# Routing table of a mixture of experts built on the chip, in place of a scatter to HBM

## The reference, cut to what matters

```python
x = x + scan_layer(layernorm(x))                      # 8 sequences of 1024 tokens
xt = layernorm(x).reshape(8192, 256)
scores = softmax(xt @ gate_w.T)                       # 15 experts
topk_w, topk_idx = top_k(scores, 3); topk_w /= topk_w.sum(-1)
comb = zeros(8192, 15); comb[t, topk_idx] += topk_w
h  = einsum('td,efd->etf', xt, fc1_w) + fc1_b         # 15 x 512
a  = gelu(h[..., 256:]) * h[..., :256] * geglu_mult
y  = einsum('etd,te->td', a @ fc2_w.T + fc2_b, comb)
ys = shared_expert(xt)                                # the same form, 512 wide
out = x + y + ys
```

## Time and profile before

| | us |
|---|---|
| median of 3 runs | 1831.01 (1828.75 to 1833.40) |
| the profiled execution | 1831.13 |
| its span | 1829.3 |
| busy in the span: PE, DVE, ACT, POOL | 1484.2, 1081.9, 873.3, 1123.2 |
| POOL's scatters into the table, 192 | 193.7 busy, 152.7 idle before them |
| mean granted clock of TensorE | 0.915 |

### The profile page before, as it was taken

One profiled execution on the slowest core, in us unless ns is written; L12 is line 12 of the kernel. 1 busy time (PEld: TensorE's weight loads), 2 busy tenths in 40 slices (PEclk: granted clock), 3 DMA queues, 4 the chain that ended last, 5 costly groups with the idle time before them and its releaser, 6 DMA issues. The chain is left out here.

```text
span 1829.3 us, 24446 instructions
## 1 busy us (share of the span) xinstructions
PE 1484.2 (81%) x5592; PEld 894.7 (49%) x5592; DVE 1081.9 (59%) x2159; ACT 873.3 (48%) x1490; POOL 1123.2 (61%) x1005
## 2 busy tenths in 40 slices
PE   6893667677677499666994399999999999996997
PEld 3432444445444244333453166666666666664565
DVE  5655999999999354133653144444444444442698
ACT  6887989988998232112220133333333333332110
POOL 6887888888886256456675366666666666662000
PEclk9996888888889699888997599999999999998999
DMA  4333233333231589999897022222222222224895
GB/s 146 132 110 137 71 127 115 127 115 110 99 126 59 189 116 130 103 98 138 99 95 96 29 89 88 87 87 89 87 87 88 89 84 90 89 87 155 313 347 210
DMA packets 75225, 216.47 MB, mean 118 GB/s; under 512 B 19926, under 2 KB 20950, under 8 KB 75120
## 3 DMA queue, kind: packets, MB, share of 16 engines
q1 hardware_dynamic: 41664, 133.23, 27.4%
q0 software_dynamic: 27904, 61.06, 10.6%
q10 hardware_dynamic: 5552, 20.86, 8.0%
HBM read 147.89 MB, written 67.21 MB: 118 GB/s over the span
## 5 line engine op out<-in xcount | busy, mean ns | idle before, releaser
L1766 PE MATMUL bank<-arena_dt,xgT 128*128 x832 | 393.8, 596 | 0.1
L738 POOL TENSOR_TENSOR state<-arena_x,b_all 128x1024 f32<-128x1024 f32 x128 | 301.8, 2370 | 67.0 <-issue 64.5
L762 PE MATMUL bank<-ident,state 128*128 128x128 f32 x1024 | 202.4, 332 | 147.4 <-ACT scaled L675 71.2
L1721 POOL DMA_INDIRECT choice_out<-ye,ids x208 | 205.2, 987 | 163.3 <-DVE ye L1874 159.9
L817 DVE TENSOR_TENSOR_SCAN state<-bank,state 128x1024 f32<-128x1024 f32 x128 | 291.5, 2278 | 5.0 <-POOL state L738 4.9
L1860 DVE TENSOR_TENSOR hid<-bank,arena_x 128x512 f32<-128x512 f32 x208 | 143.8, 692 | 251.0 <-PE bank L1766 251.0
L1316 POOL DMA_INDIRECT row_table<-choice_all,row_i x192 | 193.7, 1009 | 152.7 <-DMA row_table<-choice_all,row_i 85.2
L762 PEld LDWEIGHTS bank<-ident,state 128*128 128x128 f32 x1024 | 158.0, 211 | 197.6 <-DVE state L817 111.2
L1712 POOL DMA_INDIRECT xg<-x_norm,tokens x208 | 201.3, 968 | 72.9 <-issue 60.9
L1832 ACT ACTIVATE gluT<-bank 128x256 f32<-128x256 f32 x208 | 79.9, 384 | 321.8 <-PE bank L1775 321.8
L1783 PE MATMUL bank<-arena_x,gluT 128*128 x832 | 213.9, 380 | 0.0
(11 more groups left out here) (180 smaller groups left out, 2202.4 us busy)
## 6 DMA issues: line engine op xcount, KB each, us to landing
b_all<-bc_rows SPq DMA_DIRECT2D x64, 512.0 KB, 3.6
arena_x<-choice_out SPq DMA_DIRECT2D x16, 1536.0 KB, 10.2
xin<-in_x SPq DMA_DIRECT2D x16, 512.0 KB, 3.6
x_skip<-xin SPq DMA_DIRECT2D x16, 512.0 KB, 2.6
y_acc<-x_skip SPq DMA_DIRECT2D x8, 1024.0 KB, 6.7
x_mid<-y_acc SPq DMA_DIRECT2D x8, 1024.0 KB, 6.5
arena_x<-x_mid SPq DMA_DIRECT2D x16, 512.0 KB, 27.3
x_norm<-arena_x SPq DMA_DIRECT2D x16, 512.0 KB, 30.8
```

The lines of the kernel that those rows point to most:

```text
L738: pool.tensor_tensor(state[j % STATES][:, :, here], gT[:, :, b, here], b_all[j % BUFS][:, here].unsqueeze(1).to_broadcast([P, KD, TH]), AL ...
L762: last = pe.transpose(bank[:, TURN + (BY_PE * j + q) % 2, i * D + k * P:i * D + (k + 1) * P], state[j % STATES][:, k, t // GT * CH + t % G ...
L1721: pool.indirect_dma_start(out=choice_out, out_offset=bass.IndirectOffsetOnAxis(ap=ids[:, j % 2, j // 2:j // 2 + 1], axis=0), in_=ye[c][:], ...
L1766: last = pe.matmul(bank[:, 2 + s, :], xgT[s][:, k, :], w1[:, k, ds(e_no * (2 * F), 2 * F)], start=(k == 0), stop=(k == KD - 1))
```

## The change

A row of the table is now addressed by column (expert x 8 + block of 128 rows modulo 8, 120 in all) and slot (row modulo 128). For each group DVE makes, in two halves of six choices per partition, one-hots of the slot, multiplied by the choice number plus one (`slot_hot`), and one-hots of the column (`column_hot`); `rows` splits the rank into slot and column for that, with four small instructions more; PE multiplies them, 12 products summed into a 120x128 part of PSUM bank 7 (`place`), which DVE copies out (`keep_out`). At the end, from the counts per group, DVE finds to which tile each group's column belongs (`blocks`, `tiles_of_blocks`), makes one-hots of that, and PE sums 16 products into the ids of all 208 tiles, transposed already. `scatter`, the table in HBM and its clearing are gone, and so are the two gathers and the transposes ahead of the experts. The one-hots and constants lie in b2's place and the copies partly in that of the last eighth of w1; so these two are loaded last, on ACT's queue, and the first `fc1` of the experts on PE and the first bias on DVE wait for them.

```diff
-                    def scatter(g):
-                        pool.wait_ge(rows_made, g + 1)
-                        for t in range(g * GT, (g + 1) * GT):
-                            wait(pool, c_sent[t % 4], 48 * (t // 4))
-                            for k in range(TOPK):
-                                pool.indirect_dma_start(
-                                    out=row_table, out_offset=bass.IndirectOffsetOnAxis(ap=row_i[:, t, k:k + 1], axis=0),
-                                    in_=choice_all[:, t, k:k + 1], in_offset=None).then_inc(c_sent[t % 4], 16)
@@ tensor, routing stage
-                    def rank(g):
+                    def rank(g, n_placed):
                         pe.wait_ge(seen_made, GT * (g + 1))
                         wait(pe, rank_read, g)
+                        wait(pe, out_kept, n_placed)
+                        pe.matmul(bank[0:E, 7, 64 + g:65 + g], seen[g % 2][:, 0, :], ones[:, 0:1], start=True, stop=True)
...
+                    def place(g, n_ranked):
+                        wait(pe, rank_read, n_ranked)
+                        wait(pe, out_kept, g)
+                        for h in range(2):
+                            pe.wait_ge(hots_made, 2 * g + h + 1)
+                            for m in range(HK):
+                                last = pe.matmul(bank[0:COLS, 7, P:2 * P], column_hot[h][:, m, :], slot_hot[h][:, m, :],
+                                                 start=(h == 0 and m == 0), stop=(h == 1 and m == HK - 1))
+                            last.then_inc(hots_read, 1)
...
                         for g in routed_at(q - 4):
-                            rank(g)
+                            rank(g, n_placed)
+                            n_ranked += 1
+                        for g in routed_at(q - 8):
+                            place(g, n_ranked)
+                            n_placed += 1
...
+                    pe.wait_ge(blocks_made, 1)
+                    pe.matmul(bank[0:COLS, 3, 0:GROUPS], same_expert, blocks_at[:, 0:GROUPS], start=True, stop=True)
...
+                    for g in range(GROUPS):
+                        pe.wait_ge(tiles_hot, g + 1)
+                        pe.matmul(bank[:, 5, 0:XT], ids_placed[g], tile_hot[g], start=(g == 0), stop=(g == GROUPS - 1))\
+                          .then_inc(tile_hot_read, 1)
@@ scalar, routing stage
-                            act.dma_start(b2[:, at], b2_row[at].partition_broadcast(P)).then_inc(w_loaded, 16)
-                        if q % 2 == 1 and 2 * W2N < q < 2 * W2N + 2 * W1N:
+                        if q % 2 == 1 and 2 * W2N < q < 2 * W2N + 2 * (W1N - 1):
...
+                    act.wait_ge(tile_hot_read, GROUPS)
+                    at = ds(last_w1, W1P)
+                    act.dma_start(w1[:, :, at], w1_rows[:, :, at]).then_inc(late_loaded, 16)
+                    act.wait_ge(ids_kept, 1)
+                    act.dma_start(b2[:], b2_row.partition_broadcast(P)).then_inc(late_loaded, 16)
@@ vector, routing stage
+                    def hots(g, h):
+                        dve.wait_ge(rows_made, g + 1)
+                        wait(dve, hots_read, 2 * g + h - 1)
...
+                        for m in range(HK):
+                            at = h * HK + m
+                            dve.tensor_scalar(slot_hot[h][:, m, :], number[:, 0:P], slot_block[g % 2][:, 0, at:at + 1],
+                                              choice_all[:, g * GK + at:g * GK + at + 1], ALU.is_equal, ALU.mult)
+                        dve.tensor_tensor(
+                            column_hot[h], number[:, 0:COLS].unsqueeze(1).to_broadcast([P, HK, COLS]),
+                            column[g % 2][:, h * HK:(h + 1) * HK].unsqueeze(2).to_broadcast([P, HK, COLS]), ALU.is_equal)\
+                            .then_inc(hots_made, 1)
+
+                    def keep_out(g):
+                        dve.wait_ge(hots_read, 2 * g + 2)
+                        dve.tensor_copy(ids_placed[g], bank[0:COLS, 7, P:2 * P]).then_inc(out_kept, 1)
...
+                    def tiles_of_blocks():
+                        dve.wait_ge(blocks_spread, 1)
...
+                        for g in range(GROUPS):
+                            wait(dve, tile_hot_read, g - HOTS + 1)
+                            dve.tensor_scalar(tile_hot[g], number[0:COLS, :], tile_of[:, g:g + 1], None, ALU.is_equal)\
+                               .then_inc(tiles_hot, 1)
...
+                    def read_ids():
+                        dve.wait_ge(tile_hot_read, GROUPS)
+                        table(dve.tensor_scalar(empty, bank[:, 5, 0:XT], 0.0, float(1 << 20), ALU.is_equal, ALU.mult))
+                        table(dve.scalar_tensor_tensor(ids_f, bank[:, 5, 0:XT], -1.0, empty, ALU.add, ALU.add))
+                        dve.tensor_copy(ids[:], ids_f).then_inc(ids_kept, 1)
...
                         for g in routed_at(q - 4):
                             rows(g)
+                        for g in routed_at(q - 8):
+                            keep_out(g)
...
                         for g in routed_at(q - 2):
                             choose(g)
                             if g + 3 < GROUPS:
                                 measure(g + 3)
                         if i == 3 and 0 <= j < G1:
                             add_bias(j)
+                        for h in range(2):
+                            for g in routed_at(q - 6 - h):
+                                hots(g, h)
@@ expert stage
-                    for s in range(2):
-                        pool.indirect_dma_start(
-                            out=row_ids[:, s, :], out_offset=None, in_=row_table.rearrange("(r p) o -> r (p o)", p=P),
-                            in_offset=bass.IndirectOffsetOnAxis(ap=tile_row[0:XT // 2, s:s + 1], axis=0)).then_inc(ids_loaded, 16)
...
+                    pe.wait_ge(late_loaded, 32)
                     e_of = {0: expert_of(0)}
                     fc1(0, 0, e_of[0])
...
+                    dve.wait_ge(late_loaded, 32)
                     add_bias(0, 0)
```

More of the change, by code:

```diff
@@ L1211, in model_kernel, with in_b2 @@
             wmul = sb("wmul", [P, KD, E])
-            RPP = (E + 1) * TILES // P
-            junk = sglu[1][:].rearrange("p k t -> p (k t)")[:, 0:RPP * P]
+            GK, RING_COLS = GT * TOPK, 8
+            HK, COLS = GK // 2, E * RING_COLS
+            row_i = sb("row_i", [P, GK], I32)
+            slot_block_i = sb("slot_block_i", [P, 2, GK], I32)
+            slot_block = [sb(f"slot_block{c}", [P, 2, GK]) for c in range(2)]
+            column = [sb(f"column{c}", [P, GK]) for c in range(2)]
+            room = [0]
+            def in_b2(shape, parts=P, dt=F32):
+                at, words = room[0], 1
+                for size in shape:
+                    words *= size
+                room[0] += words
+                assert room[0] <= E * D
+                return b2[0:parts, at:at + words]
+            slot_hot = [in_b2([HK, P]).rearrange("p (m c) -> p m c", m=HK) for _ in range(2)]
+            column_hot = [in_b2([HK, COLS]).rearrange("p (m c) -> p m c", m=HK) for _ in range(2)]
+            HOTS = room[0] // XT
+            tile_hot = [b2[0:COLS, (g % HOTS) * XT:(g % HOTS + 1) * XT] for g in range(GROUPS)]
+            empty, ids_f = b2[:, 0:XT], b2[:, XT:2 * XT]
+            number = in_b2([XT])
+            late_out = [in_b2([P], COLS) for _ in range(2)]
+            same_expert, lower_expert = in_b2([COLS], E), in_b2([COLS], E)
+            counts_at = in_b2([GROUPS + 1], E)
+            blocks_at = in_b2([GROUPS + 1], E)
+            first_block = in_b2([GROUPS + 1], COLS)
+            ahead_f = in_b2([GROUPS], COLS)
+            tile_of = in_b2([GROUPS], COLS)
+            ring_no = in_b2([1], COLS)
+            last_w1 = (W1N - 1) * W1P
+            ids_placed = [arena_dt[0:COLS, last_w1 + g * P:last_w1 + (g + 1) * P] for g in range(7)]
+            ids_placed += [arena_dt[0:COLS, E * 2 * F + last_w1 + g * P:E * 2 * F + last_w1 + (g + 1) * P] for g in range(7)]
+            ids_placed += late_out
+            assert len(ids_placed) == GROUPS and 7 * P <= W1P
             x2_loaded, xn2_stored, xm_loaded, stored = sems("x2_loaded", 4), sems("xn2_stored"), sems("xm_loaded"), sems("sh_stored")
@@ L1540, in choose @@
                         dve.wait_ge(index_made, g + 1)
-                        wait(dve, row_step, 2 * (g - 1))
+                        wait(dve, row_step, 5 * (g - 1))
                         dve.tensor_tensor(
@@ L1555, in rows @@
                     def rows(g):
-                        s, here = g % 2, slice(g * GT, (g + 1) * GT)
+                        s = g % 2
                         dve.wait_ge(ranked, g + 1)
[L1558 to L1562, removed]
@@ new lines, in rows @@
+                        if g == GROUPS - 1:
+                            dve.tensor_copy(counted[:], bank[:, 7, 96:96 + E])
+                            dve.tensor_scalar(counts_at[:, GROUPS:GROUPS + 1], bank[0:E, 7, 65 + g:66 + g], float(P - 1), None,
```

(19 more changed lines are left out.)

147 lines of the change are left out of this document (81 added, 66 removed).

## The result

The changed kernel takes 1865.32 us (median of 4 runs, 1861.96 to 1865.65), the kernel before in the same comparison 1829.88 (4 runs, 1825.27 to 1833.40): a ratio of 1.0191, 95% interval 1.0165 to 1.0217. The forecast was 1856 us, the range 1826 to 1882. The profiled execution takes 1861.96 us, its span is 1860.1.

What follows compares the result with a forecast made beforehand. The prediction took the loop to be bound by transfers crowded by 192 single-word scatters. Loop +26, clock +26, stage end -22.7 and expert stage -4 gave +25 us on 1831, so 1856 us, range 1826 to 1882.

Steps and rivals of the forecast that it cites:

- The expert stage: Start of the experts: first gather could come 4 us earlier, first fc1 waits for b2 instead; 4 us less.
- loop without scatters and without the table: Shared-expert loop: without the 192 scatters and their crowding it falls from 328.9 to 256 us.
- placing, rank and counts on PE: PE's added work in the loop: fourteen groups of placing products and counts, 38.7 us, bounds 30 to 52.
- waits at the placing, loop: PE waits for the second half of one-hots, late in DVE's order: fourteen waits, 58 us in all.
- clock: PE's granted clock falls to 0.50 after waits of about 4 us in the loop: 26 us, range 24 to 34.
- last shared product to next stage: End of the routing stage: next stage begins 32.5 us after the last shared product, 22.7 earlier; bounds 30 to 39.
- stage start to first fc1: Expert stage: first fc1, waiting for b2, comes 8 us after the stage's start, against 11.9 before.
- Crowding: Loop: scatters of single words slow the other transfers; 73 of 328.9 us are lost to this and return without them.
- lower bound of 0.09: PE's placing products: lowest time in us for one pass, forecast at 0.11.
- half group: DVE: six tensor_scalar and one comparison making one-hots, 2.1 us with a wait, bounds 1.4 to 3.0.
- The rival that it holds: Loop: waits of 4 us leave PE's clock at full speed; 1830 us, 1814 to 1850; chance 18%.
- well under 0.92: Sign in the loop: granted clock at 0.5 after most placing waits, its mean well under the earlier 0.92.

Runs made afterwards that it cites:

- scatters behind the loop: The kernel before with all 192 scatters moved behind the last gated product of the loop: 2022.87 us, loop 261.8 us.
- both orders: The changed kernel with half groups of one-hots ahead of choose on DVE and placing behind the slot's first layer on PE: 1776.13 us, ratio 0.9633.
- one-hots early: The changed kernel with each slot's half group of one-hots ahead of choose and the next statistics on DVE: 1790.46 us, ratio 0.9711.
- filler: The changed kernel with 9 products whose result nobody reads ahead of each group's placing on PE: 1843.12 us, ratio 0.9992.
- place late: The changed kernel with PE's placing behind the slot's first layer and DVE's copy of the sums behind the gated product: 1791.83 us, ratio 0.9722.

## Why the prediction was right

The forecast of 1856 us was 9 us low, and its way of adding up the change held but for the last term ("The expert stage", below). The terms of the sum stand here beside what the runs gave for them:

| term | predicted, us | measured, us | from |
|---|---|---|---|
| loop without scatters and without the table | 256 | 261.8 | scatters behind the loop |
| placing, rank and counts on PE | 39 | 40.3 | both orders, 302.1 - 261.8 |
| waits at the placing, loop | 58 | 56.2 | changed kernel |
| clock | 26 | 24.3 (26.1 as what is left over) | stretches at the low clock (384.4 - 302.1 - 56.2) |
| last shared product to next stage | 32.5 | 35.8 | changed kernel |
| stage start to first fc1 | 8 | 8.2, by luck | changed kernel |

The sum of the first four was 379 to 381 in the forecast; measured apart they give 382.6, and the loop took 384.4. That they add up is tested beside it: with waits but no low clock the loop should be 302.1 + 9.8 = 311.9 (one-hots early: 313.2), and with filler 302.1 + 57.9 + 6.7 = 366.7 (365.4).

**Crowding.** Right in mechanism: 67 us where 73 were forecast. The step that was off is the length of the loop without it; the walk through the orders gave 5.8 us too little. By an estimate some 10 of the 67 us are the clock's: in five stretches at the low clock PE is busy for 20.7 us in the loop before, and in none of the loop without scatters. By the Trainium skill ("DMA: Bandwidth & Descriptors", section "Issuing engines are not separate DMA queues") DMAs of all issuing engines interleave on the same 16 DMA engines. The runs agree so far: POOL's scatters, on a queue of their own, move the landing of SP's stores from 2.9 to 9.2 us at 128 of them (800 to 900 us).

**The placing.** 24 passes took 2.78 us in one piece, 0.116 each, where 0.11 was forecast. The lower bound of 0.09 does not follow from the row given for it: 1.72 / 4 for 512 columns is 0.11 for 128.

**The wait.** It came where it was forecast, in most of the sizes forecast: 3.4 where logits stand ahead (3.6 forecast), 4.5 where transposes do (4.4), 1.7 to 4.0 in the last groups (1.9 to 4.4). The bias lies between at 749.01 us behind transposes, with 5.7, and at 833.08 behind logits, with 4.5 (6.1 to 6.4 was forecast). The longest, 6.2 at 910.74, has no bias: there a multiplication of experts' weights on DVE (L1674, 2.02 us, until 901.34) had held up the three best and `rows` ahead of the gated product, which the forecast does not name. The half group was mis-sized, 2.41 us instead of 2.1, by line and form:

```profile
L1640 DVE TENSOR_SCALAR b<-b,slot_block,choice_all 128x128 f32<-128x128 f32 x192 | 51.7, 341 | 0.0
...
L1642 DVE TENSOR_TENSOR b<-b,column 128x720 f32<-128x720 f32 x32 | 28.9, 904 | 0.0
```

A tensor_scalar with two scalars from memory takes 0.34 us, not 0.23, and six follow each other in 1.5. The wait did not grow with it, because two other errors made up for it, which is luck. From the end of PE's product DVE was at choose after some 0.7 us where 0.95 was forecast, so that its whole path took 6.65 us instead of 6.6 (at 673.92: 667.21 to 673.86); and PE's own share was longer too (first half 1.47 to 1.57 us, not 1.3). Nor did the four small instructions in rows cost nothing everywhere: at 696.59 the product ended at 688.62, but the gated product began at 689.94, behind rows. That did not show because PE's transposes there waited 1.02 us for a normalised group. For the comparison the Trainium skill ("VectorE: DVE Perf Modes", section on the TRN2 errata) gives, with its measured 150 cycles and one fp32 column a cycle, an estimated 0.906 us, and with the table's 58 an estimated 0.81; the trace has 0.904 and agrees with 150.

**The clock.** The rival that it holds is refuted by the twelve stretches and by the filler. Fourteen falls were forecast and twelve came. One sign was misread: the mean clock should have fallen "well under 0.92" and stayed at 0.92. I forgot that the kernel before lost its own share in waits of up to 16.6 us; without scatters the same loop runs at 1.00.

**The end of the stage.** 3.3 us longer than forecast, and most of that is the clock again: from 1029.7 to 1036.5 us it was low, the half placing took 2.92 us there and half a second layer 5.32, and PE was busy for 6.1 us, half of which is 3. (The 1.5 us for the barrier stood on no row; from the last id, at 1060.25, to the next stage it was 1.64.) With both orders the same path is 31.7 us, with 3.62 for that half and 1.80 instead of 2.94 for the wait in front:

```profile
943.27 1.88 PE L1434 MATMUL bank<-xnT,sw 128*128 128x512 f32 x4
...
949.76 3.62 PE L1443 MATMUL bank<-sw,sglu 128*128 128x256 f32 x16
...
976.82 1.28 ACT L1908 ACT_TABLE_LOAD   x1 [24.76 <-PEq L114]
```

I had counted waits of the loop as falls of the clock, but not those behind it.

**The expert stage.** 8.2 us to the first `fc1` where 8 was forecast, but that agreement is luck: it was not b2 that ended last. Sent at 1060.28, b2 landed at 1068.1 (8.5 us were forecast), and the first `fc1` came at 1070.10:

```profile
b<-in_fc_b ACTq DMA_DIRECT2D x1, 1920.0 KB, 7.8
```

```profile
1068.47 1.33 PE L1855 MATMUL bank<-ident,xg 128*128 128x128 f32 x4 [5.69 <-DMA xg<-x_norm,tokens]
```

PE waited for the gathered tokens, and the first of them, transposed, were copied out only at 1069.57. The first gather began 2.8 us after the stage's start, where the kernel before took 7.0. So the gather that "could come 4 us earlier" gave the gain, and the wait for b2, which the sum put in its place, kept nothing waiting here.

## What to carry to other kernels

When work moves from a DMA queue to an engine that has room on average, walk the order of the two engines that meet: this change lost 1 to 2% and the same instructions in another order win 2.9 to 3.7%, by the set of runs that the kernel before is taken from, because a half group stood behind 3.5 us of work that nobody needed yet. Price an idle gap of TensorE twice where the trace shows the granted clock falling after gaps of that size: once as wait, once as the work done at the low clock behind it. And where a term comes out as forecast, look in the trace at which wait ended last: the 8 us to the first `fc1` were right for a reason that was wrong. Ask of a crowded queue where its slack ends before planning to empty it: here a third of the scatters could have stayed in the loop for nothing (one run).

## What the runs showed that I had not expected

- The price of scatters has a knee: 0, 64, 128 and 192 in the loop give 261.8, 261.8, 276.1 and 328.9 us, at DMA shares of 0.41, 0.55, 0.84 and 0.96.
- 192 scatters with nothing beside them still keep the stage open for 308 us behind the loop, of which POOL is busy for 184.2, at a DMA share of 0.03:

```profile
910.00:1218.00 308.00, 5.36 (x24) 4.09 (x22) 9.00 (x21) 1.26 (x2) 184.18 (x192) 0.52 0.03 2
```

- The length of a wait alone did not decide whether the clock fell. Waits up to 2.69 us at the placing left it at 1.00 (one-hots early), but 2.55 (place late) and 2.30 (9 products) were followed by work at the low clock; of the fourteen from 1.67 to 6.2 us in the changed kernel twelve were followed by work at the low clock, and one of 3.38 at 887.79 us was not, though others of 3.38 were.
